# Another order of loads and of work for the first batch in a float32 kernel: relu(concat(x, mean, cond) @ W + b) + x on one core

## The chip, the core and the metric

The kernel runs on one core of a Trainium2 chip. The core has a matrix engine (TensorE, PE; its weight loads are PEld), a vector engine (VectorE, DVE), a scalar engine (ScalarE, ACT), GpSimd (POOL) and SyncE (SP), which here only issues transfers. Sixteen DMA engines move the data. The metric is the device time of one execution in microseconds, the median of several.

## The reference

Inputs: x (4, 1024, 512), cond_512 (4, 256), W (1536, 512), b (512), all float32. The two halves of the hidden vector are the same cond_512.

```
hidden = concatenate([cond, cond], axis=-1)                 # (4, 512)
x_mean = mean(x, axis=1, keepdims=True)                     # (4, 1, 512)
fused  = concatenate([x, x_mean * ones_L, hidden[:, None, :] * ones_L], axis=-1)
out    = x + relu(einsum('bld,do->blo', fused, W) + b)      # (4, 1024, 512)
```

The kernel takes W apart. W1 (rows 0 to 511) multiplies x. W2 (rows 512 to 1023) multiplies the mean over the 1024 positions, W3 (rows 1024 to 1535) the hidden vector: these two and b make one bias of 512 numbers for each batch, added inside the relu.

## The kernel before, in words

**Groups and tiles.** The 4 batches of 1024 positions are 8 groups g of 512 positions (LAST is 7). A group has 4 pieces k (128 of the 512 inputs), except group 0, which has 8 of half length: `pieces` is that list. It has 4 output tiles t of 128 outputs by 512 positions, and the last group has 8 half tiles (`tiles`, n counts them). Group g's output tile t is accumulated in bank t of `ps_y`, so there are four banks and each must be emptied before the next group's tile t begins.

**Precision.** x and W1 are each split into a high part and a rest (xh, xl, w1h, w1l), and a tile is three products for each k: w1h·xh, w1h·xl, w1l·xh (`product`, 12 matmuls of 512 columns a tile). Of W1, ACT makes the high part (L229) and POOL the rest (L201).

**A piece of x** goes: DVE turns it (32x32 transposes, `turn_x`, L300) into one of two banks of `ps_xt`; ACT rounds it to xh and sums it along the positions (`x_high`, L236, the sum is the mean's); DVE makes xl (`x_low`, L306), which frees the bank. xh and xl have four slots (SLOTS), so x may be turned three groups ahead.

**A bias** for batch b: DVE multiplies W2 with the sums (`mean_terms`, L329 to L334, the tile w2x), PE adds over the partitions (`mean_bias`, L425), and DVE adds the constant part and turns it (`sum_bias`, L346 and L349). The constant part (`ps_const`, L457, `const_row`, L372) needs W3, whose halves POOL adds (L215), cond spread on POOL (L212), and b. Both sums of a batch's two groups are needed, so the bias of batch b can be made only once its second group (2b + 1) is turned.

**A finished tile** goes: ACT adds the bias and takes the relu into `relu_t` (a ring of 8, L256), DVE turns it back (`turn_back`, L317), POOL adds it to x in place (L207; DVE in the last group, L342), SP stores a group of x (L187). Since bias 0 is late, the four tiles of group 0 are copied from `ps_y` to `relu_t` first (`save`, L242) and their relu is done there later.

**Order.** Each engine works through a list that is written out in the code. PE: group 0 with all w1h products first and the 16 w1l products last; tile 0 of group 1; then `ps_const` and the mean of batch 0; then tiles 1 to 3 of group 1; then group after group, tile t of group g behind the relu of tile t of group g - 1. The mean of batch b (b above 0) stands behind tile 2 of group 2b. DVE: groups 0 and 1, `mean_terms(0)`, one piece of group 2, bias 0, the rest of group 2, group 3, `mean_terms(1)`, and then the tiles, in which the pieces three groups ahead are interleaved. SP's loads go x0 (half), W1, x0 (half), x1, cond, W2, W3, b, x2, and x3 to x7 each behind the landing of an earlier group; ACT and POOL load the rest of W1. POOL's residual of tile n (`added`) frees a slot of `back` for `turn_back(n + 4)`.

**WARM** (L403): 14 matmuls on zeros run from the start, to 7.3 us.

## Time and profile before

| | |
|---|---|
| median of 3 runs | 114.72 us (114.51 to 115.58) |
| the profiled execution's own time | 114.67 us |
| its span | 112.9 us |
| PE busy | 99.7 us, 88% of the span |
| DVE / ACT / POOL busy | 82.9 / 48.2 / 46.0 us |
| all DMA | 20.08 MB, mean 178 GB/s |

The span is what the profile sees; 1.8 us of the execution lie outside it. Matmuls overlap, so that what one costs is the step from its start to the next one's start, 0.23 us for 512 columns and 0.12 us for 256, and not its own length. In a timeline, "idle before" is the engine's wait and the name behind the arrow what ended it.

### The profile page before, as it was taken

The page shows a single profiled execution, that of the slowest core. Times are in us where ns is not written, and L with a number is a line of the kernel's source. Part 1 is how long each engine was busy: PE and PEld are TensorE (multiplying, and loading weights), DVE is VectorE, ACT ScalarE, POOL GpSimd, SP SyncE. Part 2 cuts the span into 40 slices and gives each one's busy share as a digit, 9 for nine tenths or more (in the row PEclk, how much of TensorE's full clock was granted, in tenths as well). Part 3 has the DMA queues.
Part 4 walks back from the last instruction along what each step waited for, and adds up shares of the span by engine and source line. Part 5 has one row for each costly group of instructions (what it writes and reads, how often), then busy time and mean ns, then how long its engine had stood idle before and what let it go on. Part 6 is the DMA issues. An engine that isn't in the chain of part 4 may idle for free.

```text
span 112.9 us, 1832 instructions
## 1 busy us (share of the span) xinstructions
PE 99.7 (88%) x526; PEld 79.9 (71%) x526; DVE 82.9 (73%) x148; ACT 48.2 (43%) x118; POOL 46.0 (41%) x43
## 2 busy tenths in 40 slices
PE   5959999841999899999999999999999999999900
PEld 2319998521788588677888886888888868999900
DVE  1027849890278899999999992899999976797530
ACT  4148415910029985028738400595654006433310
POOL 5348400008000000099985620446666089980000
PEclk9999999998599999999999999999999999999995
DMA  2999999999999999994869539100391670687966
GB/s 82 259 239 231 218 203 237 339 261 219 221 219 218 223 219 222 219 217 84 198 178 226 144 76 253 43 0 0 76 252 43 160 211 6 136 234 179 255 142 171
DMA packets 36023, 20.08 MB, mean 178 GB/s; under 512 B 1968, under 2 KB 34864, under 8 KB 36016
## 3 DMA queue, kind: packets, MB, share of 16 engines
q1 hardware_dynamic: 34576, 18.69, 77.1%
q10 hardware_dynamic: 1248, 0.79, 2.6%
q0 software_dynamic: 192, 0.52, 1.8%
q8 instruction: 3, 0.05, 0.2%
q14 instruction: 4, 0.03, 0.1%
HBM read 11.60 MB, written 8.39 MB: 177 GB/s over the span
## 4 chain that ended last, share of the span: by engine, by line
PE 60%; SPq 17%; DMA 8%; ACT 5%; DVE 3%; issue 3%; DVEq 0%
PE ps_y L406 60%; DMA xa<-in_x_dram 8%; SPq L162 8%; ACT relu_t L256 3%; SPq L141 3%; SPq L171 2%; ACT xh L236 2%; SPq L175 1%; DVE ps_xt L300 1%; PE ps_mean L425 1%; SPq L169 1%; SPq L146 1%; SPq L173 1%; DVE back L317 0%; DVE xa L342 0%
## 5 line engine op out<-in xcount | busy, mean ns | idle before, releaser
L406 PE MATMUL ps_y<-xh,w1h 128*128 128x256 f32 (+2 forms) x160 | 52.9, 355 | 2.5 <-ACT xh L236 1.4
L406 PE MATMUL ps_y<-xl,w1h 128*128 128x256 f32 (+2 forms) x160 | 51.8, 348 | 0.0
L207 POOL TENSOR_TENSOR xa<-xa,back 128x512 f32 x28 | 35.7, 1303 | 37.5 <-DVE back L317 37.5
L406 PE MATMUL ps_y<-xh,w1l 128*128 (+2 forms) x144 | 50.5, 368 | 0.0
L406 PEld LDWEIGHTS ps_y<-xh,w1h 128*128 128x128 f32 x160 | 28.8, 191 | 9.2 <-issue 2.4
L256 ACT ACTIVATE relu_t<-ps_y,bias 128x512 f32<-128x512 f32 (+1 forms) x32 | 20.0, 633 | 31.2 <-DVE bias L349 22.0
L300 DVE STREAM_TRANSPOSE ps_xt<-xa 128x512 f32<-128x512 f32 (+1 forms) x36 | 22.2, 640 | 12.9 <-DMA xa<-in_x_dram 12.6
L406 PEld LDWEIGHTS ps_y<-xl,w1h 128*128 128x128 f32 x160 | 28.8, 191 | 3.6
L406 PEld LDWEIGHTS ps_y<-xh,w1l 128*128 128x128 f32 x144 | 27.2, 190 | 4.5
L236 ACT ACTIVATE xh<-ps_xt 128x512 fp32r<-128x512 f32 (+1 forms) x36 | 19.7, 548 | 23.3 <-DVE ps_xt L300 23.2
L306 DVE TENSOR_TENSOR xl<-ps_xt,xh 128x512 fp32r<-128x512 f32 (+1 forms) x36 | 22.3, 618 | 4.4 <-ACT xh L236 4.4
L317 DVE STREAM_TRANSPOSE back<-relu_t 128x512 f32<-128x512 f32 (+1 forms) x36 | 22.1, 630 | 3.9 <-ACT relu_t L256 3.7
L334 DVE SCALAR_TENSOR_TENSOR w2x<-w,bsum,w2x 128x512 f32<-128x512 f32 x12 | 9.0, 752 | 0.4
L403 PE MATMUL ps_mean<-warm 128*128 128x512 bf16 x14 | 6.1, 629 | 1.2 <-DVE warm L361 1.2
L236 ACT ACTIVATION_READ_ACCUMULATOR xh<-ps_xt 128x1 f32 x36 | 7.1, 197 | 0.0
L201 POOL TENSOR_TENSOR w1l<-w,w1h 128x512 fp32r<-128x512 f32 x4 | 5.0, 1280 | 3.9 <-ACT w1h L229 3.9
L215 POOL TENSOR_TENSOR w3sum<-w 128x1024 f32<-128x1024 f32 x1 | 2.4, 2417 | 8.2 <-DMA w<-in_L_cond_W_dram 8.2
L342 DVE TENSOR_TENSOR xa<-xa,back 128x256 f32<-128x256 f32 x8 | 5.1, 632 | 0.3
L403 PEld LDWEIGHTS ps_mean<-warm 128*128 128x128 bf16 x14 | 1.9, 145 | 4.5 <-issue 3.3
L457 PE MATMUL ps_const<-w3sum,cond_t 128*32 128x128 f32 x16 | 1.1, 419 | 4.1 <-POOL w3sum L215 4.1
L229 ACT ACTIVATE w1h<-w 128x512 fp32r<-128x512 f32 x4 | 2.4, 623 | 3.5 <-DMA w<-in_L_cond_W_dram 3.5
L457 PEld LDWEIGHTS ps_const<-w3sum,cond_t 128*32 128x32 f32 x16 | 0.7, 159 | 4.5 <-issue 4.5
(21 smaller groups left out, 19.5 us busy)
## 6 DMA issues: line engine op xcount, KB each, us to landing
xa<-in_x_dram SPq DMA_DIRECT2D x28, 256.0 KB, 6.7
out_dram<-xa SPq DMA_DIRECT2D x28, 256.0 KB, 3.5
xa<-in_x_dram SPq DMA_DIRECT2D x8, 128.0 KB, 5.9
w<-in_L_cond_W_dram SPq DMA_DIRECT2D x4, 256.0 KB, 6.8
w<-in_L_cond_W_dram SPq DMA_DIRECT2D x2, 512.0 KB, 9.7
w<-in_L_cond_W_dram POOLq DMA_DIRECT2D x4, 128.0 KB, 4.6
out_dram<-xa SPq DMA_DIRECT2D x4, 128.0 KB, 2.8
out_dram<-xa ACTq DMA_DIRECT2D x4, 128.0 KB, 2.4
```

The source lines that it names most:

```text
L162: sp.dma_start(xa[Q * j:Q * j + Q, g], xv[g, j]).then_inc(x_landed[h], 16)
L201: nc.gpsimd.tensor_tensor(as_tiles(w1l[:, k]), by_tile(w1[:, k]), as_tiles(w1h[:, k]), ALU.subtract).then_inc(w1l_ready, 1)
L207: nc.gpsimd.tensor_tensor(rows, rows, back[:, t], ALU.add).then_inc(added, 1)
L236: nc.scalar.activation(xh[:, g % SLOTS, k, l:l + nl], ps_xt[:, n % XT_BANKS, 0:nl], ACT.Copy, accum_out=xsum[:, part, k:k + 1]).then_inc(x ...
L256: nc.scalar.activation(relu_t[:, slot, 0:nl], products, ACT.Relu, bias=bias[:, g // H, t, g // H:g // H + 1]).then_inc(relu_done, 1)
L300: nc.vector.transpose(ps_xt[:, n % XT_BANKS, 0:nl], xa[:, g, l // Q:(l + nl) // Q, Q * k:Q * k + Q]).then_inc(xt_ready, 1)
L306: nc.vector.tensor_tensor(xl[:, g % SLOTS, k, l:l + nl], ps_xt[:, n % XT_BANKS, 0:nl], xh[:, g % SLOTS, k, l:l + nl], ALU.subtract).then_i ...
L317: nc.vector.transpose(back[:, t, 0:nl // Q], relu_t[:, n % RELU_RING, 0:nl].rearrange("p (lb om) -> p lb om", om=Q)).then_inc(turned_back, 1)
L334: nc.vector.scalar_tensor_tensor(out=w2x[:], in0=w2[:, k], scalar=bsum[:, k:k + 1], in1=w2x[:], op0=ALU.mult, op1=ALU.add).then_inc(w2x_st ...
L342: nc.vector.tensor_tensor(rows, rows, back[:, t, 0:nl // Q], ALU.add).then_inc(last_added, 1)
L403: nc.tensor.matmul(ps_mean[:], warm[:, 0:P], warm[:], start=True, stop=True)
L406: return nc.tensor.matmul(ps_y[:, t, ls], lhs, rhs, start=start, stop=stop, skip_group_check=True)
```

## The change

Five things are changed together.

1. **Loads at the start.** x0 and W1 are issued by SP (partition quadrants 0 and 1, `LOW`) and ACT (quadrants 2 and 3, `HIGH`); POOL issues none. W1 comes in pieces k = 0, k = 1, and k = 2 and 3. SP then loads alone: cond, x1, x2, W2, W3, b, x3 to x7, with no wait for a landing between them.
2. **cond** is loaded as 4 DMAs of 4 rows of 256 bytes into a zeroed tile and turned by DVE, instead of one DMA of 8-byte runs and a copy on POOL.
3. **Group 0 on PE**: the w1l products are interleaved with the others, as 32 matmuls of 256 columns instead of 16 of 512, and the last piece is done tile by tile.
4. **All 8 tiles of batch 0** (groups 0 and 1) are saved to `relu_t` (`SAVED`), so group 2 waits for `y_saved` and not for a relu.
5. **Order.** DVE turns group 2 before `mean_terms(0)`. PE does `ps_const` and the mean of batch 0 after all of group 1, and the mean of batch 1 in the middle of tile 3 of group 2, where it waits for bias 0 and w2x. Later means stand where they stood.

```diff
         @block.sync
         def _(sp):
...
-            load_x0(sp, 0)
-            load_w1(sp, 1, range(0, 2), w1_landed)
-            load_x0(sp, 1)
-            load_x(1, 1)
-            sp.dma_start(cond_c[:], cv).then_inc(cond_landed, 16)
-            for j in ORDER:
-                sp.dma_start(w2[Q * j:Q * j + Q], wv[1, j]).then_inc(w2_landed, 16)
+            load_x0(sp, 0, LOW)
+            load_w1(sp, 0, 1, LOW)
+            load_w1(sp, 1, 2, LOW)
+            load_w1(sp, 2, NK, LOW)
+            load_x0(sp, 1, LOW)
+            sp.wait_ge(cond_zeroed, 1)
+            for j in range(NQ):
+                sp.dma_start(cond_c[Q * j:Q * j + B], cv[j].rearrange("b (m k) -> b m k", k=CK)).then_inc(cond_landed, 16)
+            load_x(sp, 1, ORDER)
+            load_x(sp, 2, ORDER)
+            load_w2(sp, ORDER)
             for r in range(2):
                 sp.dma_start(w3[:, r], w3v[r]).then_inc(w3_landed, 16)
...
+            for g in range(3, G):
+                load_x(sp, g, ORDER)
...
         @block.scalar
         def _(act):
-            load_w1(act, 0, range(0, 2), w1_landed)
+            load_x0(act, 0, HIGH)
             act.wait_ge(ones_set, 1)
             nc.scalar.activation(act_warm[:], ones[:, 0:1], ACT.Relu)
+            load_w1(act, 0, 1, HIGH)
+            load_w1(act, 1, 2, HIGH)
+            load_w1(act, 2, NK, HIGH)
+            load_x0(act, 1, HIGH)
...
             def relu(n):
                 g, l, nl, t = tiles[n]
                 products, slot = ps_y[:, t, l:l + nl], n % RELU_RING
-                if g == 0:
+                if n < SAVED:
                     act.wait_ge(y_saved, n + 1)
                     products = relu_t[:, slot]
...
+            save(0)
+            x_high(pieces_to(H) - 1)
+            for n in range(1, NK):
+                save(n)
+            n_x = pieces_to(H)
+            x_high(n_x)
+            x_high(n_x + 1)
+            save(NK)
...
         @block.vector
...
-            turn_and_split(0, pieces_to(H))
+            turn_and_split(0, pieces_to(1))
+            dve.wait_ge(cond_landed, 16 * NQ)
+            nc.vector.transpose(cond_t[:], cond_c[:].rearrange("p m k -> p k m")).then_inc(cond_spread, 1)
...
+            turn_x(pieces_to(H))
+            turn_and_split(pieces_to(H), pieces_to(H + 1))
             mean_terms(0)
...
         @block.tensor
...
             for t in range(NK):
                 pe.wait_ge(y_saved, t + 1)
                 tile(1, 1, t)
...
+            pe.wait_ge(cond_spread, 1)
+            pe.wait_ge(w3_added, 1)
...
+            mean_bias(0)
+
+            for t in range(NK):
+                pe.wait_ge(y_saved, NK + t + 1)
+                for k in range(NK):
...
+                    if t == NK - 1 and k == NK // 2:
+
+                        pe.wait_ge(bias_ready, 1)
+                        mean_bias(1)
+                    last = product(H % SLOTS, k, t)
```

**On DVE, behind group 1** (the first x_low pair below is the end of group 1). Before, the mean of batch 0 comes straight behind it and x2 is turned around bias 0:

```order
L306 TENSOR_TENSOR xl<-ps_xt,xh 128x512 [waits xh_ready] x2
L323 TENSOR_TENSOR xsum<-xsum 128x4
L329 TENSOR_TENSOR bsum<-xsum 128x4 [waits halves_summed,w2_landed]
L331 TENSOR_SCALAR w2x<-w,bsum 128x512 [waits bsum_ready]
L334 SCALAR_TENSOR_TENSOR w2x<-w,bsum,w2x 128x512 [waits w2x_step] x3
L300 STREAM_TRANSPOSE ps_xt<-xa 128x512 [waits xl_ready,x_landed0]
L306 TENSOR_TENSOR xl<-ps_xt,xh 128x512 [waits xh_ready]
L372 TENSOR_TENSOR const_row<-ps_const,b_row 128x128 [waits b_landed,const_summed]
L346 SCALAR_TENSOR_TENSOR bias_row<-ps_mean,const_row 128x128 [waits mean_done,const_ready]
L349 STREAM_TRANSPOSE bias<-bias_row 128x128 [waits bias_summed]
L300 STREAM_TRANSPOSE ps_xt<-xa 128x512 [waits xl_ready] x2
```

With the change, from the end of group 2 on (its first row is the last x_low pair of group 2; line numbers are the changed kernel's):

```order
L303 TENSOR_TENSOR xl<-ps_xt,xh 128x512 [waits xh_ready] x2
L320 TENSOR_TENSOR xsum<-xsum 128x4
L326 TENSOR_TENSOR bsum<-xsum 128x4 [waits halves_summed,w2_landed]
L328 TENSOR_SCALAR w2x<-w,bsum 128x512 [waits bsum_ready]
L331 SCALAR_TENSOR_TENSOR w2x<-w,bsum,w2x 128x512 [waits w2x_step] x3
L372 TENSOR_TENSOR const_row<-ps_const,b_row 128x128 [waits b_landed,const_summed]
L343 SCALAR_TENSOR_TENSOR bias_row<-ps_mean,const_row 128x128 [waits mean_done,const_ready]
L346 STREAM_TRANSPOSE bias<-bias_row 128x128 [waits bias_summed]
L297 STREAM_TRANSPOSE ps_xt<-xa 128x512 [waits xl_ready,x_landed3]
```

All four pieces of x2 have moved ahead of the mean, and what follows bias 0 is now group 3, behind its landing.

**On PE, where the constant part stands.** Before, behind the last product of tile 0 of group 1:

```order
L406 MATMUL ps_y<-xh,w1l 128x512
L457 MATMUL ps_const<-w3sum,cond_t 32x128 [waits w3_added,cond_spread]
L457 MATMUL ps_const<-w3sum,cond_t 32x128 x7
L425 MATMUL ps_mean<-w2x,ones 32x128 [waits w2x_step]
L425 MATMUL ps_mean<-w2x,ones 32x128 x3
L406 MATMUL ps_y<-xh,w1h 128x512 [waits y_saved]
```

With the change, behind the last product of tile 3 of group 1 and ahead of group 2:

```order
L406 MATMUL ps_y<-xh,w1l 128x512
L471 MATMUL ps_const<-w3sum,cond_t 32x128 [waits w3_added,cond_spread]
L471 MATMUL ps_const<-w3sum,cond_t 32x128 x7
L425 MATMUL ps_mean<-w2x,ones 32x128 [waits w2x_step]
L425 MATMUL ps_mean<-w2x,ones 32x128 x3
L406 MATMUL ps_y<-xh,w1h 128x512 [waits xl_ready,y_saved]
```

36 matmuls of 512 columns (tiles 1 to 3 of group 1) now stand ahead of the wait for W3.

**On PE, tile 3 of group 2**, which has a wait in its middle that it did not have:

```order
L406 MATMUL ps_y<-xh,w1l 128x512
L425 MATMUL ps_mean<-w2x,ones 32x128 [waits w2x_step,bias_ready]
L425 MATMUL ps_mean<-w2x,ones 32x128 x3
L406 MATMUL ps_y<-xh,w1h 128x512
L406 MATMUL ps_y<-xl,w1h 128x512
L406 MATMUL ps_y<-xh,w1l 128x512
```

Before, the same four mean matmuls of batch 1 stood ahead of tile 3.

## Rows read from the trace of the kernel before

**Rows 1.** The page's busy times and one group of it; PE's waits (total, times, longest).

```profile
PE 99.7 (88%) x526; PEld 79.9 (71%) x526; DVE 82.9 (73%) x148; ACT 48.2 (43%) x118; POOL 46.0 (41%) x43
...
L229 ACT ACTIVATE w1h<-w 128x512 fp32r<-128x512 f32 x4 | 2.4, 623 | 3.5 <-DMA w<-in_L_cond_W_dram 3.5
...
PE ps_const L457 <- POOL w3sum L215: 4.1, 1, 4.1
PE ps_y L406 <- ACT xh L236: 1.4, 1, 1.4
```

**Rows 2.** The chain that ended last: start us, us, what.

```profile
39.13 8.46 PE ps_y L406 x36
47.60 0.36 PE ps_mean L425 x8
...
50.97 19.34 PE ps_y L406 x84
...
107.51 0.48 ACT relu_t L256
```

**Rows 3.** Timeline of PE: start us, us, engine, line, tiles, count, idle before.

```profile
1.21 6.11 PE L403 MATMUL ps_mean<-warm 128*128 128x512 bf16 x14 [1.21 <-DVE warm L361]
...
8.74 0.74 PE L406 MATMUL ps_y<-xh,w1h 128*128 128x256 f32 x4 [1.42 <-ACT xh L236]
...
20.85 0.50 PE L406 MATMUL ps_y<-xh,w1h 128*128 128x512 f32 x1 [0.48 <-ACT relu_t L242]
...
27.93 1.11 PE L457 MATMUL ps_const<-w3sum,cond_t 128*32 128x128 f32 x16 [4.07 <-POOL w3sum L215]
...
29.39 0.80 PE L406 MATMUL ps_y<-xh,w1h 128*128 128x512 f32 x1
...
31.17 0.39 PE L406 MATMUL ps_y<-xl,w1h 128*128 128x512 f32 x1
```

**Rows 4.** Timeline of DVE, ACT and POOL: the first users of x1, W3 and x2.

```profile
16.65 1.32 DVE L300 STREAM_TRANSPOSE ps_xt<-xa 128x512 f32<-128x512 f32 x2 [1.37 <-DMA xa<-in_x_dram]
...
20.20 0.59 ACT L242 ACTIVATE relu_t<-ps_y 128x512 f32<-128x512 f32 x1
...
25.36 2.42 POOL L215 TENSOR_TENSOR w3sum<-w 128x1024 f32<-128x1024 f32 x1 [8.21 <-DMA w<-in_L_cond_W_dram]
...
30.29 0.73 DVE L300 STREAM_TRANSPOSE ps_xt<-xa 128x512 f32<-128x512 f32 x1 [4.70 <-DMA xa<-in_x_dram]
```

**Rows 5.** Windows: stretch, length, busy by engine, PE clock, DMA share, GB/s.

```profile
15.00:16.00 1.00, 1.00 (x11) 1.00 (x10) 0.28 (x1) 0.00 (x0) 0.00 (x0) 1.00 1.33 181
...
26.00:30.00 4.00, 2.07 (x26) 1.63 (x27) 0.00 (x0) 0.00 (x0) 1.78 (x1) 0.70 1.22 220
```

**Rows 6.** Timeline of DVE from bias 0 to bias 1, and ACT's relu behind it.

```profile
32.38 0.28 DVE L372 TENSOR_TENSOR const_row<-ps_const,b_row 128x128 f32<-128x128 f32 x1
...
33.25 1.27 DVE L300 STREAM_TRANSPOSE ps_xt<-xa 128x512 f32<-128x512 f32 x2
...
38.28 1.31 DVE L300 STREAM_TRANSPOSE ps_xt<-xa 128x512 f32<-128x512 f32 x2
...
43.91 0.15 DVE L329 TENSOR_TENSOR bsum<-xsum 128x4 f32<-128x4 f32 x1
...
46.86 2.48 DVE L317 STREAM_TRANSPOSE back<-relu_t 128x512 f32<-128x512 f32 x4
...
49.98 0.69 ACT L256 ACTIVATE relu_t<-ps_y,bias 128x512 f32<-128x512 f32 x1 [6.14 <-DVE bias L349]
```

**Rows 7.** Timeline: SP's queue, which issues transfers, and ACT's table load.

```profile
0.76 1.85 SPq L141 DMA_DIRECT2D xa<-in_x_dram  x4
...
1.68 1.28 ACT L224 ACT_TABLE_LOAD   x1 [1.68 <-PEq L498]
...
5.60 4.66 SPq L162 DMA_DIRECT2D xa<-in_x_dram  x4
10.30 1.02 SPq L169 DMA_DIRECT2D cond_c<-in_cond_dram  x1
```

More of the change, by code:

```diff
@@ L62, in build @@
     tiles += [(LAST, l, HL, t) for l in (0, HL) for t in range(NK)]
+    SAVED = H * NK
     def steps_of_x(n, ahead):
-        return 1 if SLOTS <= tiles[n][0] + ahead < G else 0
+        return 1 if SLOTS <= n // NK + ahead < G else 0
     xv = x.rearrange("b (h lb lm) (j e) -> (b h) j lm lb e", h=H, lm=Q, j=NQ)
@@ L136, in build, with load_x0, load_x, load_w1 @@
         turned_back, added, last_added = sem("turned_back"), sem("added"), sem("last_added")
-        def load_x0(eng, half):
+        def load_x0(eng, half, quadrants):
             lbs = slice(half * LB // 2, (half + 1) * LB // 2)
-            for j in ORDER:
+            for j in quadrants:
                 eng.dma_start(xa[Q * j:Q * j + Q, 0, lbs], xv[0, j, :, lbs]).then_inc(x0_landed[half], 16)
-        def load_w1(eng, half, quadrants, landed):
-            ks = slice(half * NK // 2, (half + 1) * NK // 2)
+        def load_x(eng, g, quadrants):
             for j in quadrants:
-                eng.dma_start(w1[Q * j:Q * j + Q, ks], wv[0, j, :, ks]).then_inc(landed[half], 16)
+                eng.dma_start(xa[Q * j:Q * j + Q, g], xv[g, j]).then_inc(x_landed[g], 16)
+        def load_w1(eng, first, end, quadrants):
+            for j in quadrants:
+                eng.dma_start(w1[Q * j:Q * j + Q, first:end], wv[0, j, :, first:end]).then_inc(w1_landed[first], 16)
+        def load_w2(eng, quadrants):
+            for j in quadrants:
+                eng.dma_start(w2[Q * j:Q * j + Q], wv[1, j]).then_inc(w2_landed, 16)
         def store_last(eng, quadrants):
@@ L434, in _ @@
                         pe.wait_ge(w1h_ready, k + 1)
+                    if half == 1 and k == NK - 1:
+                        pe.wait_ge(xl_ready, NK * H)
+                        for t in range(NK):
+                            mm(t, ls, w1h[:, k, t], xh[:, 0, k, ls])
+                            mm(t, ls, w1h[:, k, t], xl[:, 0, k, ls])
+                            mm(t, ls, w1l[:, k, t], xh[:, 0, k, ls], stop=True).then_inc(y_ready, 1)
+                        break
                     for t in range(NK):
@@ L440, in _ @@
                         mm(t, ls, w1h[:, k, t], xl[:, 0, k, ls])
-            for t in range(NK):
-                for k in range(NK):
-                    if t == 0:
-                        pe.wait_ge(w1l_ready, k + 1)
-                    last = mm(t, slice(0, NL), w1l[:, k, t], xh[:, 0, k], stop=(k == NK - 1))
-                last.then_inc(y_ready, 1)
+                    if half == 0 and k > 0:
+                        group0_low(half, k - 1)
+                    elif half == 1:
+                        group0_low(half, k)
+                if half == 0:
+                    group0_low(half, NK - 1)
             for t in range(NK):
@@ L474, in _ @@
                     tile(H * b + 1, (H * b + 1) % SLOTS, t)
-            even_group(B - 1)
+                for t in range(NK):
+                    pe.wait_ge(relu_done, NK * (H * b + 1) + t + 1)
+                    tile(H * b + H, (H * b + H) % SLOTS, t)
+                    if t == 2:
+                        pe.wait_ge(bias_ready, b + 1)
+                        mean_bias(b + 1)
             for n, (g, l, nl, t) in enumerate(tiles):
```

133 lines of the change are left out of this document (52 added, 81 removed).

## The prediction

> **What bounds the kernel now.** I read the page first: PE is busy for 99.7 of 112.9 us and nothing else comes near [rows 1]. The chain that ended last says the same: from 50.97 us on it is PE without a gap down to 107.5, and then relu, turn and store of the last half tile [rows 2]. So behind 50.97 only PE's own work counts, and the change adds and removes none there. What can be won lies ahead of it, and the list of PE's waits shows where: 4.1 us for POOL's sum of W3, and 1.4 us at the start for the first xh [rows 1]. The timeline gives the gaps a place. PE starts real work at 8.74, though its zero matmuls end at 7.32 (1.21 + 6.11), waits 0.48 before 20.85, and waits 4.07 before 27.93 [rows 3]. After that long gap it is slow as well: the granted clock is 0.70 on the mean of 26 to 30 us [rows 5], 16 + 8 small matmuls take 1.46 us (27.93 to 29.39) and the next four big ones 1.78 us (29.39 to 31.17) [rows 3]. At full pace these are 24 x 0.045 = 1.08 us (eight take 0.36 [rows 2]) and 4 x 0.23 = 0.92 us. The clock's fall cost 1.24 us.
>
> Last, what do the waits hang on? DMA moves 220 GB/s at share 1.22 even while PE idles, in 26 to 30, so it isn't resting [rows 5], and the first users of x1 (16.65), W3 (25.36) and x2 (30.29) start as these land [rows 4]. The first 35 us are a race with one full stream.
>
> **The change part by part.** I walk PE through the changed order, with durations of this trace, up to the start of group 3, which in the old trace is at 50.97.
>
> Loads at the start. Group 0 can start when x0's first half and W1's k = 0 are there. Best case is 7.35, behind the zero matmuls. Worst case: ACT's ten issues, at the pitch of SP's (1.85 us for four), and the table load between them (1.3) [rows 7] hold ACT to 0.76 + 4.6 + 1.3 = 6.7, and two xh and one w1h, at most 0.62 each [rows 1], make it 8.6. Either way group 0 is 96 matmuls of 256 columns at 0.12 = 11.5 us, and ends at 18.9 to 20.1; the 16 more weight loads hide in that pitch. But PE doesn't go on then: tile 0 of group 1 waits for the copy of tile 0, which ACT has behind three xh of group 1, and that copy starts at 20.20 because x1 lands at 16.65 [rows 4]. The three MB up to x1 are the same as before. I move x1's landing by 0 to 0.3 us and take 0.1. The start's gain ends there: group 1 starts at 20.75 instead of 20.85.
>
> The Trainium skill, "DMA: Bandwidth & Descriptors", section "Issuing engines are not separate DMA queues", says that DMAs of several engines share the same 16 DMA engines and that several issuers save only issue time. By that rule x1 gains nothing from the second queue, as in my sum; a gain of the start that is kept is a rival below.
>
> cond. Its 512 runs of 8 bytes show as the dip at 15 to 16 us: 181 GB/s at share 1.33 [rows 5]. 41 GB/s missing over 1 us, and a smaller dip behind it, are 0.25 us of the stream. Sixteen runs of 256 bytes cost next to nothing: W2, W3 and x3 land 0.25 us sooner, bounds 0 and 0.5. The new wait for cond on DVE stands ahead of x1's first piece; it is issued in front of x1 and so comes ahead of it. The turn of 64 columns costs at most the 0.3 of bias' turn and hides in DVE's idle 1.37 us before 16.65 [rows 4]. If cond came late, DVE would hold x1 and all behind it.
>
> Group 1. 48 matmuls at 0.23 = 11.05 us: 20.75 to 31.8. Its four tiles are saved by ACT, which has only x2's four pieces beside them in that time; group 2's tiles find their banks free.
>
> W3 now stands behind x2. A group of x is 1.05 MB, at 220 GB/s 4.77 us [rows 5]. So W3 is there at 25.36 + 4.77 - 0.25 = 29.9, its sum is done 2.42 later at 32.3 [rows 4], and the constant part starts at 32.45 (0.15 behind it as now). PE waits 0.65 instead of 4.07, too short for the clock to fall, going by the gap of 1.42 that did no such thing [rows 3]. Then 24 small matmuls at full pace: 33.55. w2x of batch 0 is ready: x2 lands near 16.6 + 4.77 = 21.3, and with 5.63 for a group and 2.95 for the mean (below) DVE has x1 split at 22.2, x2 at 27.8 and w2x at 30.9.
>
> Group 2 up to the middle of tile 3: 42 matmuls, 9.7 us, 33.6 to 43.3. There PE waits for bias 0 (below: 34.5, no wait) and for w2x of batch 1.
>
> The DVE chain now decides. const_row to the next turn is 0.87 us (32.38 to 33.25) [rows 6], so bias 0 is there at 34.5. x3 closes the same amount of data as before: 30.27 + 4.77 = 35.0, less 0.25 and a little: L = 34.7. From the first turn of a group to the next bsum DVE took 5.63 us (38.28 to 43.91) with ACT mostly free. With relus between, three pieces took 5.03 (33.25 to 38.28), or 6.7 for four [rows 6]. Now a relu stands between any two xh; it is nearer the first, since only one stands there and not two, and I take 6.0. bsum at 40.7. From there the old trace needs 2.95 to the first turn_back (46.86) and, over four turn_backs and bias 1, 6.76 until the relu that frees bank 0 is done (49.98 + 0.69 = 50.67) [rows 6]. The changed order on this stretch is the same. So w2x is ready at 43.65 (PE waits 0.35 for it), PE does the mean (0.36) and six matmuls (1.4) and ends group 2 at 45.4; the relu is done at 40.7 + 6.76 = 47.5, and PE starts group 3 at 47.5 after 2.1 us idle.
>
> Behind that the order on all engines is as before, and DVE, which leads this restart, keeps its place ahead of PE. The stores begin sooner, behind the same loads.
>
> **The sum.** 50.97 - 47.5 = 3.5 us less. Cross-check: groups 1 and 2 are 96 matmuls of 0.23 and 24 + 8 small ones, 23.5 us of work. The old stretch 20.85 to 50.97 is 30.1, so 6.6 of it is waiting: 4.07, the clock's 1.24, and shorter ones. The new one is 23.5 + 0.65 + 0.35 + 2.1 = 26.6, from 20.75 to 47.4. Against the profiled run's 114.67 that is 111.2; its time is within 0.05 of the median.
>
> Bounds of the unknown: L 34.2 to 35.3; the pass 5.63 to 6.7. Group 3 starts at 46.6 to 48.8, the time is 110.3 to 112.5.
>
> **The rivals.**
> - *The clock falls in group 2's wait* (2.1 us). 4.07 idle did it, 1.42 did not [rows 3]; this one is between. Price 1.24 as above: 112.4. Chance 0.12.
> - *The data come sooner.* If the second queue brought x0, W1 and x1 forward as much as PE's gap of 1.42 [rows 1], all landings move by that and the chain with them: 111.2 - 1.4 = 109.8. For it: four transfers are issued at once at the start, two by each engine. Against: SP's first issue is at 0.76 in both, and four are out by 2.6 in the old trace already [rows 7]. Chance 0.15.
> - *W3 decides, not x3.* If W3 or its sum is late by 1 us more than I have it, bias 0 holds DVE instead of x3: 34.5 + 1 + 6.0 + 6.76 = 48.3, 112.0, inside the range. Chance 0.13.
> - *x3 is late, slower than before.* x3 to x7 are issued with no wait for a landing, so x4's traffic may run beside x3's. If x3 lands a whole load (4.77) later, group 3 starts at 52.2 and the time is 115.9. It decides from L = 39.3 on. For it: SP needed 4.66 us for four issues at 5.60 [rows 7], so the queue was full. Against: x1 and x2 landed in their turn although W2 and others stood behind them. Chance 0.04.
> - *Nothing is won*: DVE's chain is the limit in both kernels, and bsum would have to come at the old 43.91 [rows 6], 3.2 later than in my sum, say by a landing of x3 at 37.9; 114.4. Chance 0.04.
>
> **How the numbers follow.** The forecast has 0.52. Range: 109.6 (data sooner) to 112.8 (clock falls, and a little late). A measurement of this kernel can tell 1% from no change. Under 113.6 are all but the last two, and some part of these: faster 0.91, same 0.05, slower 0.04.
>
> **What the changed profile would show.** PE: group 1 at 20.4 to 20.9, with idle time before it for ACT's copy; ps_const at 32 to 33 after under 1.5 us of waiting; a short wait in tile 3 of group 2; a wait near 2 us for the relu before group 3 at 46.6 to 48.8, in a chain that runs through DVE and x3's landing; no window at clock 0.5. From there 56.5 us of gapless PE. Wrong would be: group 1 before 20 (data sooner), PE gapless up to group 3, or a DVE that waits for cond.

## The result, and the profile after

The changed kernel takes 111.15 us (median of 4, 109.17 to 112.69), against 114.62 us (114.12 to 115.58, 4) for the kernel before on the same chip. The ratio is 0.955, with a 95% interval of 0.943 to 0.967, so faster; it rests on the changed kernel's two executions with a mean granted clock of 0.989 and 0.996 (109.17 and 109.98; the other two, at 0.976, took 112.31 and 112.69, see a2), and puts the time at 0.955 x 114.62 = 109.5 us. The direction was forecast, and the mechanism except for the loads at the start; by this ratio the time lies 1.7 us below the 111.2 and just below the range's low end of 109.6.

The profiled execution took 109.98 us with a span of 108.2, which is 4.7 less than before. First the page of the changed kernel, with its busy times (share of the span) and instruction counts:

```profile
PE 97.4 (90%) x542; PEld 79.7 (74%) x542; DVE 85.4 (79%) x149; ACT 50.4 (47%) x122; POOL 43.5 (40%) x38
```

PE is busier by share, and 2.3 us less in all, because no stretch ran at half clock (which the prediction prices at 1.24 us) and the zero matmuls took 4.99 us for 6.11 [rows 3]. The chain of work that ended last, of the changed kernel (start us, us, what):

```profile
33.59 0.72 ACT relu_t L252
...
39.88 0.76 DVE w2x L331
...
42.21 2.40 DVE back L314 x4
45.25 0.70 ACT relu_t L252
46.25 19.33 PE ps_y L406 x84
...
102.78 0.48 ACT relu_t L252
```

As before, the end is one gapless PE [rows 2]. It begins at 46.25 instead of 50.97, 4.72 sooner, and that is the whole gain: 50.97 to 107.51 were 56.5 us, 46.25 to 102.78 are 56.5 too. Ahead of it the chain runs through DVE and ACT, not through PE. PE's timeline of the changed kernel (idle time before a row, and what ended it, in brackets) has the places that the prediction names:

```profile
7.07 0.71 PE L406 MATMUL ps_y<-xh,w1h 128*128 128x256 f32 x4 [0.89 <-ACT w1h L227]
...
18.76 0.28 PE L406 MATMUL ps_y<-xh,w1l 128*128 128x256 f32 x1
19.59 0.50 PE L406 MATMUL ps_y<-xh,w1h 128*128 128x512 f32 x1 [0.55 <-ACT relu_t L239]
...
31.04 0.67 PE L471 MATMUL ps_const<-w3sum,cond_t 128*32 128x128 f32 x16 [0.28 <-POOL w3sum L210]
32.29 0.43 PE L425 MATMUL ps_mean<-w2x,ones 128*32 128x128 f32 x8 [0.58 <-DVE w2x L331]
```

The wait of 4.07 for POOL's sum [rows 3] has shrunk to 0.28. The wait of 0.58 for w2x was not in my sum. DVE's timeline of the changed kernel, from x1 to bias 1, with the relu of ACT that frees bank 0:

```profile
15.40 1.32 DVE L297 STREAM_TRANSPOSE ps_xt<-xa 128x512 f32<-128x512 f32 x2 [0.64 <-DMA xa<-in_x_dram]
...
27.67 4.56 DVE L331 SCALAR_TENSOR_TENSOR w2x<-w,bsum,w2x 128x512 f32<-128x512 f32 x3
32.15 0.28 DVE L372 TENSOR_TENSOR const_row<-ps_const,b_row 128x128 f32<-128x128 f32 x1
32.86 0.29 DVE L343 SCALAR_TENSOR_TENSOR bias_row<-ps_mean,const_row 128x128 f32<-128x128 f32 x1 [0.43 <-PE ps_mean L425]
...
33.52 1.32 DVE L297 STREAM_TRANSPOSE ps_xt<-xa 128x512 f32<-128x512 f32 x2
...
39.17 0.15 DVE L326 TENSOR_TENSOR bsum<-xsum 128x4 f32<-128x4 f32 x1
...
42.12 2.48 DVE L314 STREAM_TRANSPOSE back<-relu_t 128x512 f32<-128x512 f32 x4
44.53 0.25 DVE L343 SCALAR_TENSOR_TENSOR bias_row<-ps_mean,const_row 128x128 f32<-128x128 f32 x1
44.82 0.31 DVE L346 STREAM_TRANSPOSE bias<-bias_row 128x128 f32<-128x128 f32 x1
```

```profile
45.25 0.69 ACT L252 ACTIVATE relu_t<-ps_y,bias 128x512 f32<-128x512 f32 x1 [4.27 <-DVE bias L346]
```

x1 is turned at 15.40, where it was 16.65 [rows 4]: 1.25 us sooner, against the 0.1 that I had taken. x3 is turned at 33.52 without a wait, right behind bias 0. And three instructions that took 0.75 each before take 4.56 together: the second of them takes 2.99, beside POOL's sum of the halves of W3.

```profile
28.45 2.99 DVE L331 SCALAR_TENSOR_TENSOR w2x<-w,bsum,w2x 128x512 f32<-128x512 f32 x1
```

```profile
28.50 2.40 POOL L210 TENSOR_TENSOR w3sum<-w 128x1024 f32<-128x1024 f32 x1 [16.26 <-DMA w<-in_L_cond_W_dram]
```

The windows of the changed kernel (stretch, length, busy by engine, PE clock, DMA share, GB/s) show where the data gained:

```profile
5.00:10.00 5.00, 4.10 (x28) 3.11 (x27) 2.65 (x8) 3.43 (x12) 2.86 (x3) 1.00 1.06 298
15.00:16.00 1.00, 1.00 (x10) 1.00 (x9) 0.60 (x1) 0.00 (x0) 0.00 (x0) 1.00 1.23 227
```

and the same of the kernel before, of the first stretch:

```profile
5.00:10.00 5.00, 3.58 (x16) 1.87 (x15) 2.00 (x6) 2.64 (x8) 2.50 (x2) 1.00 1.11 239
```

In 5 to 10 us DMA moved 298 GB/s instead of 239. That is 0.30 MB more, and at the 225 GB/s of the stretch behind it 1.3 us of the stream.

### The profile page after: what moved, and what is told of

Same layout as the page of the kernel before. It is cut to its first block, busy times and chain, and to the rows that moved or that the text cites. A ratio compares the mean times of both kernels' runs of the same rounds, so it can differ in the third digit from the quotient of the medians.

```text
span 108.2 us, 1750 instructions
## 1 busy us (share of the span) xinstructions
PE 97.4 (90%) x542; PEld 79.7 (74%) x542; DVE 85.4 (79%) x149; ACT 50.4 (47%) x122; POOL 43.5 (40%) x38
## 4 chain that ended last, share of the span: by engine, by line
PE 53%; DVE 18%; ACT 10%; DMA 7%; SPq 6%; issue 2%; ACTq 0%; DVEq 0%
PE ps_y L406 52%; DMA xa<-in_x_dram 7%; DVE w2x L331 6%; ACT xh L234 5%; ACT relu_t L252 3%; DVE ps_xt L297 3%; DVE xl L303 3%; DVE back L314 3%; SPq L152 2%; SPq L144 2%; ACT relu_t L239 1%; SPq L148 1%; SPq L177 1%; PE ps_mean L425 1%; DVE w2x L328 1%
## 5 line engine op out<-in xcount | busy, mean ns | idle before, releaser
L406 PE MATMUL ps_y<-xh,w1l 128*128 128x256 f32 (+2 forms) x160 | 51.9, 347 | 0.0
L406 PEld LDWEIGHTS ps_y<-xh,w1l 128*128 128x128 f32 x160 | 28.7, 189 | 3.9
L252 ACT ACTIVATE relu_t<-ps_y,bias 128x512 f32<-128x512 f32 (+1 forms) x28 | 17.3, 626 | 29.4 <-DVE bias L346 20.1
L331 DVE SCALAR_TENSOR_TENSOR w2x<-w,bsum,w2x 128x512 f32<-128x512 f32 x12 | 11.3, 938 | 0.4
L252 ACT ACTIVATE relu_t<-relu_t,bias 128x512 f32<-128x512 f32 x8 | 5.4, 720 | 2.2 <-DVE bias L346 2.2
L239 ACT ACTIVATE relu_t<-ps_y 128x512 f32<-128x512 f32 x8 | 4.5, 596 | 3.7 <-PE ps_y L406 3.7
L403 PE MATMUL ps_mean<-warm 128*128 128x512 bf16 x14 | 5.0, 533 | 1.2 <-DVE warm L358 1.2
L343 DVE SCALAR_TENSOR_TENSOR bias_row<-ps_mean,const_row 128x128 f32<-128x128 f32 x4 | 1.1, 281 | 3.3 <-PE ps_mean L425 3.3
```

What stands on the lines that cost most here:

```text
L239: nc.scalar.activation(relu_t[:, n % RELU_RING], ps_y[:, n % Y_BANKS], ACT.Copy).then_inc(y_saved, 1)
L252: nc.scalar.activation(relu_t[:, slot, 0:nl], products, ACT.Relu, bias=bias[:, g // H, t, g // H:g // H + 1]).then_inc(relu_done, 1)
L331: nc.vector.scalar_tensor_tensor(out=w2x[:], in0=w2[:, k], scalar=bsum[:, k:k + 1], in1=w2x[:], op0=ALU.mult, op1=ALU.add).then_inc(w2x_st ...
L403: nc.tensor.matmul(ps_mean[:], warm[:, 0:P], warm[:], start=True, stop=True)
L406: return nc.tensor.matmul(ps_y[:, t, ls], lhs, rhs, start=start, stop=stop, skip_group_check=True)
```

## The experiments

The theories. **A, my walk**: PE's stretch ahead of group 3 is set by DVE's chain from the landing of the data, and only the size of one landing was off. **B, the data**: the new start brings x1 and all behind it sooner by 1 us or more. **C, two engines on one memory port**: DVE's long w2x instruction is long because POOL adds W3 at the same time. **D, the clock**: the wait before group 3 lets it fall in some executions. Each ratio below is to the kernel before on the same chip, with its 95% interval. Where not said otherwise, the edit is made to the changed kernel.

**a0_again, the changed kernel once more, on the chip of the next ones.**

> The changed kernel once more, on the chip of the three runs beside it. Its executions so far took 109.17 and 109.98 us at a mean granted clock of 0.989 and 0.996, and 112.31 and 112.69 us at 0.976. If the clock can fall in PE's 1.83 us wait before group 3, the times here split again into about 109.2 to 110 and 112.3 to 112.7. If the split was chance of that chip, they lie together within 0.5 us.

Measured: 110.42 us (109.12 to 111.11, 4), ratio 0.960 (0.952 to 0.967). x1 is turned at 14.90 and group 3 starts at 45.41. The gain repeats, and so does x1's early landing. The four times fit neither outcome: they spread over 2.0 us, but the two at the lower clock (0.969 and 0.977) took only 110.92 and 111.11.

**a5_old_start, the old loads of x0 and W1 and the old cond** (parts 1 and 2 undone, with ACT's old order of its first roundings, except that x1 to x7 stay in the new order):

```diff
-            load_x0(sp, 0, LOW)
-            load_w1(sp, 0, 1, LOW)
-            load_w1(sp, 1, 2, LOW)
-            load_w1(sp, 2, NK, LOW)
-            load_x0(sp, 1, LOW)
...
+            load_x0(sp, 0, ORDER)
+            load_w1(sp, 1, range(0, 2), w1_landed)
+            load_x0(sp, 1, ORDER)
             load_x(sp, 1, ORDER)
+            sp.dma_start(cond_c[:], cv).then_inc(cond_landed, 16)
...
+            load_w1(pool, 0, range(2, NQ), w1_q23_landed)
```

> The changed kernel with parts 1 and 2 undone at the start: x0, W1 and cond are loaded as before (cond behind x1, copied by POOL); the order x1, x2, W2, W3, b, x3, the saved tiles, group 0's matmuls and the places of the means are the changed kernel's. This is the kernel that my sum described, in which x1 lands when it did before: x1 at 16.3 to 16.7, the constant part at 32 to 33, group 3 near 47.5, 111.0 to 111.5 in the executions whose clock holds. If the start's parts are worth nothing, it is 109.2 to 110.0 like the changed kernel.

Measured: 112.72 us (111.49 to 115.67, 10), ratio 0.979 (0.974 to 0.984). Its timeline of PE and DVE:

```profile
32.58 0.67 PE L470 MATMUL ps_const<-w3sum,cond_t 128*32 128x128 f32 x16 [0.79 <-POOL w3sum L214]
...
47.60 0.49 PE L405 MATMUL ps_y<-xh,w1h 128*128 x1 [1.88 <-ACT relu_t L253]
```

```profile
16.40 1.32 DVE L298 STREAM_TRANSPOSE ps_xt<-xa 128x512 f32<-128x512 f32 x2 [1.01 <-DMA xa<-in_x_dram]
...
34.86 1.32 DVE L298 STREAM_TRANSPOSE ps_xt<-xa 128x512 f32<-128x512 f32 x2 [0.57 <-DMA xa<-in_x_dram]
```

With the old start, x1 lands within 0.15 of my 16.55, x3 at 34.86 where I had 34.7, the constant part starts at 32.58 where I had 32.45, and group 3 at 47.60 where I had 47.5. So the walk from x1 on was right (A), and what it lacked was the start (B). The time is less clean: of the ten executions one kept its clock (0.998), and it took 111.97 for the 111.0 to 111.5 expected; the traced one took 112.92, of which 1.6 are the clock's (see a2), so 111.3 without. As for size, the new start is worth 0.979 - 0.955 = 2.4% or some 2.7 us by the two ratios, whose intervals together span about 0.7 to 4.7 us, and 1.35 us by the two traces (47.60 against 46.25). The rest between these two would be the clock, whose mean is under 0.983 in nine of this kernel's ten executions, against four of eight of the changed kernel's. Why it falls more often here isn't shown.

**b1_start_loads, the kernel before with the new loads of x0 and W1 alone; b3_loads_cond, with the new cond too.**

```diff
-            load_x0(sp, 0)
-            load_w1(sp, 1, range(0, 2), w1_landed)
-            load_x0(sp, 1)
+            load_x0(sp, 0, LOW)
+            load_w1(sp, 0, 1, LOW)
+            load_w1(sp, 1, 2, LOW)
+            load_w1(sp, 2, NK, LOW)
+            load_x0(sp, 1, LOW)
...
-            load_w1(pool, 0, range(2, NQ), w1_q23_landed)
-            load_w1(pool, 1, range(2, NQ), w1_q23_landed)
```

> The kernel before with one part of the change: x0 and W1 issued by SP and ACT, W1 in three pieces, nothing issued by POOL; all else, the old order of loads too, as before. In the kernel before the first user of x1 starts at 16.65, in the changed one at 15.40. If the start of the loads did that, x1 is turned at 15.4 to 15.7 here, W3's sum starts near 24.2 instead of 25.36, and the time falls by about 1.2 us (113.4). If cond's 8-byte runs (issued behind x1) or another part did it, x1 is turned at 16.4 to 16.7 and the time falls by 0.3 or less.

> The kernel before with two parts of the change: the new loads of x0 and W1, and cond as four small DMAs in front of x1, turned by DVE; the old order of all else. With the start's loads alone x1 was turned at 16.31 us, though 3.36 MB had come by 15.0, more than the 3.15 MB up to x1. If the 512 runs of 8 bytes that stand behind x1 in the queue hold x1's last packets up, x1 is turned at 15.0 to 15.6 here as in the changed kernel (15.40), and W3's sum starts by 24.6. If cond's form costs only its 0.25 us of transfer, behind x1, x1 is turned at 16.2 to 16.4 again. The wait for W3 stays (4 to 5 us) in both, and the clock falls as before, so the time is 113 to 114.

Measured: b1 114.55 us (113.04 to 115.49, 4), ratio 0.985 (0.976 to 0.993). b3 112.31 us (112.09 to 113.91, 5), ratio 0.982 (0.973 to 0.991), less than the 113 to 114 expected. The first use of x1 in b1 and then in b3, in DVE's timeline:

```profile
16.31 1.32 DVE L301 STREAM_TRANSPOSE ps_xt<-xa 128x512 f32<-128x512 f32 x2 [1.08 <-DMA xa<-in_x_dram]
```

```profile
15.73 1.32 DVE L300 STREAM_TRANSPOSE ps_xt<-xa 128x512 f32<-128x512 f32 x2 [0.86 <-DMA xa<-in_x_dram]
```

**a3_pool_w1, W1's upper quadrants issued by POOL again instead of ACT**, the new cond kept:

```diff
+            load_w1(pool, 0, 1, HIGH)
+            load_w1(pool, 1, 2, HIGH)
+            load_w1(pool, 2, NK, HIGH)
...
-            load_w1(act, 0, 1, HIGH)
-            load_w1(act, 1, 2, HIGH)
-            load_w1(act, 2, NK, HIGH)
```

> The changed kernel with one thing undone: quadrants 2 and 3 of W1 are issued by POOL again, in the new pieces. If POOL's queue cost the 1.15 us by which x1 comes sooner in the changed kernel, x1 is turned at 16.2 or later and the time rises by about 1 us. If cond's form or place did it, x1 stays at 15.2 to 15.6, and the time within 0.4 us of the changed kernel.

Measured: 111.51 us (110.59 to 113.14, 4), ratio 0.973 (0.957 to 0.989), whose interval overlaps the changed kernel's. x1 is turned at 15.92, between the two outcomes, and DMA moved 269 GB/s in 5 to 10 us. Group 3 starts at 47.33, 1.1 later than in the changed kernel.

Nine traces have the new loads and the new cond (after, a0, a1, a2, a6, b3, and a7, c1, c2 below). They turn x1 at 14.90 to 15.73, with a middle of 15.34. The old start (before, a5, b4) turns it at 16.65, 16.40 and 16.63, so that the two groups don't meet: the new start as a whole brings x1 about 1.2 us sooner. How this divides is much less sure. a3, which issues from POOL, is at 15.92, outside the nine by 0.2 only; b1, which has the old cond, is at 16.31. Each is one execution, against a scatter of 0.8. The bytes say more of the issuer: by 15.0 us, 3.10 to 3.14 MB had been moved with the old start, 3.23 in a3, and 3.36 to 3.57 in all that have POOL issue nothing.

Of cond they say little. Against b3, b1's x1 is 0.6 later. But SP issues the old cond only at 9.39 in b1, and by 9.4 b1 had already moved 0.11 MB less than b3 (2.08 against 2.19), which is half a microsecond of the stream. b1 had moved 3.68 MB when x1 was turned, more than the changed kernel's 3.48; but b3, without the 8-byte runs, had moved 3.69. So these runs don't show that cond's old form costs more than the 0.25 that the prediction gave it, nor that it holds x1's last packets back.

The later landings scatter as well. POOL starts its sum of W3 at 25.36 in the kernel before and at 23.97 in b4, which has the same loads. In b1, where 24.2 was expected if the start decided, it is 26.14; in b3 it is 24.92.

**a6_old_group0, the old order of group 0's w1l products** (part 3 undone):

```diff
-                    if half == 0 and k > 0:
-                        group0_low(half, k - 1)
-                    elif half == 1:
-                        group0_low(half, k)
...
+            for t in range(NK):
+                for k in range(NK):
...
+                    last = mm(t, slice(0, NL), w1l[:, k, t], xh[:, 0, k], stop=(k == NK - 1))
```

> The changed kernel with group 0's matmuls in the old order (all w1h products first, then 16 w1l products of 512 columns). PE starts group 1 when ACT has copied tile 0, and ACT has three pieces of x1 ahead of that copy, so x1's landing decides and not PE's order: group 1 starts 4.2 us behind the first turn of x1 as in the changed kernel (19.59 for 15.40), and the time is 109.1 to 110.2 in the executions whose clock holds. If the interleaving matters, group 1 starts later against x1 by more than 0.3 us and the time rises by as much.

Measured: 110.06 us (109.43 to 110.61, 4), ratio 0.959 (0.952 to 0.967), the same as a0's 0.960 within the intervals. Group 1 starts at 19.54 there and at 19.59 in the changed kernel. Part 3 is worth nothing that these runs show, because group 1 waits for ACT's copy behind x1, and group 3 for DVE. Parts 1 and 2 on the old kernel (b3) have a ratio of 0.982, parts 3 to 5 on the old start (a5) 0.979, all five 0.955. What parts 4 and 5 are worth singly isn't tested.

**a7_w_first, W2, W3 and b loaded ahead of x2, as the kernel before had it**:

```diff
             load_x(sp, 1, ORDER)
-            load_x(sp, 2, ORDER)
             load_w2(sp, ORDER)
...
-            for g in range(3, G):
+            for g in range(2, G):
```

> The changed kernel with one thing undone: SP loads W2, W3 and b ahead of x2. DVE still turns x2 ahead of the mean. x2 then lands near 28.9, DVE has it split at 34.5 and w2x of batch 0 at 37.5, and PE, through with group 1 at 30.7, waits near 6 us for it, long enough for the clock to fall (0.50 in a window behind it). Group 2 starts near 37.9 and not 32.64, group 3 near 51, and the time is 114.5 to 116.5. If the order of the loads matters little since the queue is full anyway, it stays under 111.

Measured: 116.66 us (116.19 to 117.83, 4), ratio 1.018 (1.010 to 1.027), 1 to 3% slower than before and just above the range expected. A row of DVE's timeline and one of PE's:

```profile
29.09 1.32 DVE L296 STREAM_TRANSPOSE ps_xt<-xa 128x512 f32<-128x512 f32 x2 [8.26 <-DMA xa<-in_x_dram]
```

```profile
38.08 0.66 PE L424 MATMUL ps_mean<-w2x,ones 128*32 128x128 f32 x8 [7.01 <-DVE w2x L330]
```

and a window of it, with the clock in the third column from the end:

```profile
34.00:42.00 8.00, 3.92 (x16) 2.87 (x17) 6.69 (x14) 3.93 (x11) 0.00 (x0) 0.50 1.19 231
```

DVE's new order (x2 turned ahead of the mean) makes everything wait for x2, so the load order has to go with it. Behind the wait of 7.01 for w2x PE runs at half clock until past 42 us, and group 3 starts at 52.75, for the 51 expected. With DVE's order as it is, the place of x2 in the stream decides between a ratio of 0.955 and one of 1.018.

**a1_w3_on_pe, no sum on POOL: PE multiplies both halves of W3 instead**, with 32 small matmuls for 16:

```diff
-            nc.gpsimd.tensor_tensor(w3sum[:], w3[:, 0], w3[:, 1], ALU.add).then_inc(w3_added, 1)
...
-                for k in range(CK):
+                for r in range(2):
+                    for k in range(CK):
```

> The changed kernel without POOL's sum of the halves of W3: PE multiplies cond with both halves (32 small matmuls instead of 16). In the changed kernel one of the three multiply-adds of w2x takes 2.99 us instead of 0.75, from 28.45 on, and POOL's sum runs from 28.50 to 30.90. Port theory (DVE and POOL both read two SBUF tiles, and the one that comes second waits): all twelve multiply-adds take 0.75, w2x of batch 0 is ready at 29.2, the mean follows the constant part with no wait, bias 0 is ready near 32.6 and not 33.5, and the time falls by 0.3 to 0.9 us, less if x3 has not landed by then. DMA theory (the load of W3 and b slows DVE): one multiply-add still takes near 3 us and bias 0 comes at 33.5.

Measured: 110.24 us (110.06 to 112.00, 6), ratio 0.956 (0.950 to 0.961). From its timelines:

```profile
27.30 2.33 DVE L329 SCALAR_TENSOR_TENSOR w2x<-w,bsum,w2x 128x512 f32<-128x512 f32 x3
32.89 0.29 DVE L370 TENSOR_TENSOR const_row<-ps_const,b_row 128x128 f32<-128x128 f32 x1 [3.26 <-PE ps_const L470]
```

```profile
30.39 2.13 PE L470 MATMUL ps_const<-w,cond_t 128*32 128x128 f32 x29
```

The three DVE instructions are short again, which bears C out, but the 0.3 to 0.9 us expected don't show (a0 on the same chip has 110.42 and 0.960): PE now spends over 2 us on the constant part, DVE waits 3.26 for it, and bias 0 comes at 33.85 instead of 33.5.

**c1_bias_first, DVE makes bias 1 behind the first turn_back instead of behind the fourth.** In the changed kernel w2x of batch 1 is ready at 42.12 and PE's mean is done in 42.40 to 42.75, but DVE turns four tiles back (2.48 us) before it makes the bias that group 3 waits for.

```diff
+                if n == 1:
+                    sum_bias(1)
...
-                    if n // NK % H == H - 1 and n // NK // H + 1 < B - 1:
+                    if n // NK % H == H - 1 and 1 < n // NK // H + 1 < B - 1:
```

> The changed kernel with one move on DVE: bias 1 is made behind the first turn_back and not behind the fourth. PE waits 1.83 us for the relu of tile 0 of group 2, and that waits for bias 1. Three turn_backs are 1.8 us, so that bias 1 should be there 1.6 us sooner (it then waits for the mean's matmuls) and PE goes on nearly without a wait: 108.2 to 108.6 with an unbroken clock, and no slower executions, since the wait in which the clock fell is gone. Rival: DVE is the next limit; what PE gains it loses at the mean of batch 2, which DVE has ready only 1.8 us early now, and the time stays near 109.5.

Measured: 108.79 us (107.98 to 109.91, 4), ratio 0.948 (0.935 to 0.960). Its timeline of DVE, and of PE:

```profile
42.06 0.70 DVE L314 STREAM_TRANSPOSE back<-relu_t 128x512 f32<-128x512 f32 x1
42.89 0.29 DVE L343 SCALAR_TENSOR_TENSOR bias_row<-ps_mean,const_row 128x128 f32<-128x128 f32 x1
43.21 0.31 DVE L346 STREAM_TRANSPOSE bias<-bias_row 128x128 f32<-128x128 f32 x1
```

```profile
44.65 0.49 PE L408 MATMUL ps_y<-xh,w1h 128*128 x1 [0.24 <-issue]
...
47.86 0.50 PE L408 MATMUL ps_y<-xh,w1h 128*128 x1 [0.21 <-ACT relu_t L252]
```

The wait of 1.83 before group 3 is gone and PE starts it 1.6 us sooner. Of this 0.5 is lost again by the mean of batch 2, 0.2 of it in the wait at 47.86; the time is a little above the 108.2 to 108.6 expected. That the DVE chain decided group 3's start (A) is shown by this. It is the fastest of all kernels here, by its median and by its ratio, though the intervals of its ratio and the changed kernel's (0.943 to 0.967) overlap.

**c2_w3_behind, c1 with POOL's sum of W3 held until w2x of batch 0 is done.**

```diff
+            pool.wait_ge(w2x_step, NK)
             nc.gpsimd.tensor_tensor(w3sum[:], w3[:, 0], w3[:, 1], ALU.add).then_inc(w3_added, 1)
```

> The kernel with bias 1 behind the first turn_back, and POOL's sum of W3 held until DVE has w2x of batch 0. With no overlap all twelve multiply-adds should take 0.75 us (port theory); w2x is ready near 29.5, the sum runs 29.6 to 32.0, and the constant part and the mean follow each other at 32.1 to 33.0. That is 0.2 us later than the 32.76 at which the mean ends with the overlap, so the time should be within 0.4 us of the kernel with bias 1 moved (107.98 to 108.79). If a multiply-add still takes 2.7 to 3 us, POOL's sum isn't its cause.

Measured: 109.72 us (109.00 to 111.47, 4), ratio 0.952 (0.945 to 0.960). Its timelines:

```profile
27.78 2.33 DVE L332 SCALAR_TENSOR_TENSOR w2x<-w,bsum,w2x 128x512 f32<-128x512 f32 x3
```

```profile
30.19 2.35 POOL L211 TENSOR_TENSOR w3sum<-w 128x1024 f32<-128x1024 f32 x1 [18.07 <-DVE w2x L332]
```

```profile
32.69 0.67 PE L474 MATMUL ps_const<-w3sum,cond_t 128*32 128x128 f32 x16 [1.77 <-POOL w3sum L211]
```

The same POOL instruction, put behind instead of beside, and DVE's three take 2.33 instead of 4.56. With a1 this settles C. The time, expected within 0.4 us of c1's, is 0.9 above it: PE waits 1.77 for the sum that was held, the constant part starts at 32.69 and not at 32.1, and group 3 at 45.61 instead of c1's 44.65.

Other traces have the two side by side, and the order decides who is stretched. A multiply-add that runs when POOL starts keeps its 0.75 (a2, a3, a5, a6, b4, c1, and before, at 24.83). The next one, issued during POOL's sum, takes 2.75 to 2.83 (a0, a2, a5, a6, b4, c1). POOL's instruction in turn takes 2.61, 2.74 and 2.75 where a running multiply-add still had 0.36 or more to go (a6, a3, c1), and 2.34 to 2.43 in the others. Only in the changed kernel's trace does the long multiply-add begin first, by 0.05.

**a2_fill, 8 zero matmuls in PE's wait before group 3**, so that the wait is filled whatever its cause. Nothing reads their results.

```diff
+            for _n in range(8):
+                nc.tensor.matmul(ps_const[:], warm[:, 0:P], warm[:], start=True, stop=True)
```

> The changed kernel with 8 matmuls on zeros (512 columns bf16, into the bank of the constant part, read by nobody) in PE's wait before group 3, which is 1.83 us; at 0.22 us each they end 0.3 us before PE is released. If the slower executions (112.3 to 112.7) are those in which the clock falls in that wait, they vanish here: all executions at 109.2 to 110.2, mean granted clock at 0.985 or above in all. If they come from elsewhere they stay, at 0.976, and the median doesn't move.

Measured: 110.40 us (109.86 to 110.64, 4), ratio 0.957 (0.951 to 0.963). All four clocks are at 0.987 or above, as expected, but three of the times lie above the 110.2, and the median is a0's 110.42: the filling gains nothing here. Theory D is about single executions. Those of the changed kernel took 109.17 and 109.98 at a mean granted clock of 0.989 and 0.996, and 112.31 and 112.69 at 0.976; a1's took 110.1 to 110.4 four times at 0.991 to 0.998 and 111.89 and 112.00 at 0.977 and 0.979. The trace of a1 is one in which it fell behind the wait. Its timeline, with its windows (clock in the third column from the end):

```profile
46.53 0.50 PE L404 MATMUL ps_y<-xh,w1h 128*128 x1 [1.77 <-ACT relu_t L250]
...
47.61 0.63 PE L404 MATMUL ps_y<-xh,w1h 128*128 x1
48.03 0.63 PE L404 MATMUL ps_y<-xl,w1h 128*128 x1
```

```profile
48.00:50.00 2.00, 2.00 (x6) 1.58 (x5) 2.00 (x5) 1.75 (x6) 2.00 (x3) 0.50 1.14 214
```

Behind 1.77 us of idling the step from matmul to matmul is 0.43 (1.2 GHz) instead of 0.23 until 50.17. Twelve matmuls take 46.53 to 50.97, 4.44, which is 1.6 more than twelve at 0.23 and the 0.1 of a first one. a5's trace shows the same behind 1.88 us. The traces of the changed kernel, a0, a3 and a6 have waits of 1.77 to 1.87 at the same place and stay at 2.4 GHz, and so do b4 and c2 behind 1.84 and 1.77 us elsewhere. So such a wait lets the clock fall or not. Over all executions of kernels with the wait before group 3 (the changed kernel, a0, a1, a3, a5, a6), 17 of 32 have a mean clock of 0.982 or less. Of the twelve without it (a2, c1, c2) one has, at 0.980 and 111.47 us, in c2, which has its wait of 1.77 before the constant part. That fits D. But only a1's and a5's traces show where the clock fell; for the changed kernel's own four low executions it is inferred from their mean, and a0's are less cleanly split than a1's.

**b4_fill_before, the kernel before with 18 zero matmuls in its 4.07 us wait.** This asks what the clock's fall, which I had priced at 1.24 us, was worth.

```diff
+                    for _n in range(18):
+                        nc.tensor.matmul(ps_const[:], warm[:, 0:P], warm[:], start=True, stop=True)
```

> The kernel before with 18 matmuls on zeros (3.9 us at full clock, results read by nobody) in PE's wait of 4.07 us for W3's sum. The wait stays, the granted clock should not fall: no window at 0.5 between 27 and 33, and the time lower by the clock's price, which I put at 1.24 us: 113.2 to 113.6 for 114.6 to 115. If the slow matmuls behind the wait had another cause, the time stays or rises by the few tenths by which the zeros may run over.

Measured: 114.57 us (113.26 to 115.45, 10), ratio 0.995 (0.990 to 1.000). From PE's timeline and windows:

```profile
23.73 4.06 PE L453 MATMUL ps_const<-warm 128*128 128x512 bf16 x18
...
38.84 0.49 PE L406 MATMUL ps_y<-xh,w1h 128*128 x1 [1.84 <-ACT relu_t L256]
```

```profile
26.00:30.00 4.00, 4.00 (x39) 2.44 (x37) 1.63 (x3) 0.00 (x0) 0.32 (x1) 1.00 1.22 224
```

The clock stayed at 1.00 where it had been 0.70 [rows 5], PE was through group 1 sooner, and then it waited 1.84 for the relu before group 2, where the kernel before has 0.50. Group 2 starts at 38.84 instead of 39.13, and DVE turned x2 at 29.99 instead of 30.29, sooner by as much. DVE's chain from x2's landing decided that start all along, and the clock's fall was hidden behind it.

## Why the prediction was right and wrong

**What bounds the kernel.** Right. The gapless stretch behind group 3's start is 56.5 us in both, and the gain is the shift of its start.

**Loads at the start.** This is the step that failed, in the sentence "I move x1's landing by 0 to 0.3 us and take 0.1" and in the one behind it, "The start's gain ends there". It measured 1.25 us. The term was taken from "The three MB up to x1 are the same as before". The bytes are the same, the rate is not: 239 GB/s in 5 to 10 us of the kernel before, where the changed kernel moves 298. I read rates only at 15 and at 26 us and held the stream to be full. The window of 5 to 10 us would have warned me by its DMA share, 1.11 for 1.22 later, but not by its rate, which is above the later 222; that 298 could be moved there, only a run could show. Group 1 was to start when the copy of tile 0 let it, and it did so at 19.59 with 0.55 idle, instead of at 20.75, since the copy hangs on x1 as I had said. "Group 1 before 20 (data sooner)" was the prediction's own sign for this. Group 0 started at 7.07, ahead of my best case of 7.35, because the zero matmuls ended at 6.18 and not at 7.32; nothing came of that.

Beside this step stood a rule of the Trainium skill, "DMA: Bandwidth & Descriptors", section "Issuing engines are not separate DMA queues": several issuers save only issue time. The traces do not bear it out for this start as a whole: by 9.4 us it had moved 2.08 to 2.21 MB in ten traces (2.04 in a3, where POOL issues half of W1), against 1.85 to 1.88 with the old one. As the pieces and their order changed too, how much is the issuers' isn't separated.

**cond.** I took 0.25 (bounds 0 and 0.5) for all landings behind it, by the bandwidth that its dip takes. The runs don't measure it: b1's x1 is 0.6 behind b3's, but 0.5 of that lay there before the old cond was issued. The new wait of DVE for cond costs nothing: it turns cond at 14.52 in the changed kernel, and x1 only at 15.40.

**Group 1, W3 and the constant part.** Right in kind. W3 was used at 28.50 where I had 29.9, 1.4 sooner, and the wait was 0.28 for my 0.65. The clock held. But this landing scatters: the sum starts between 26.91 and 29.07 in five traces with these loads (after, a0, a2, a6, c1). Under the old start, a5 has 32.58 for my 32.45.

**w2x of batch 0.** I had it ready at 30.9 and PE without a wait. It was ready at 32.2, though DVE had turned x2 sooner than I thought, since the POOL sum of W3 now ran beside it. One SCALAR_TENSOR_TENSOR took 2.99 us instead of 0.75 while POOL's 2.40 ran, and PE waited 0.58. Before, the sum came at 25.36 [rows 4], when DVE's last multiply-add (24.83 to 25.58) was already running. I had moved both and not looked at whether they now meet. What it cost is an estimate: from the start of the constant part to bias_row it is 1.82 us here and 1.07 in c2, so it held bias 0 up by at most 0.75, and by less if x3 landed after 32.8.

The Trainium skill has this case: "SBUF — State Buffer", section "Who interferes with whom", says that a DVE instruction with two SBUF inputs contends with a GpSimd instruction that reads SBUF, and that the issue order decides who blocks. The traces agree: 2.99 beside the sum, 0.75 without (a1, c2), and in six more the one issued second is the one that is stretched (see c2).

**x3 and the pass.** I had DVE wait for x3 until 34.7. It didn't wait: bias 0 held it until 33.52. So in the rival's words W3's side decides and not x3, only sooner than in my numbers, because both had come sooner. The two are close: in a2 and a5 DVE waits 0.61 and 0.57 for x3. My low bound for group 3, 46.6, took x3 at 34.2 and forgot that my own bias 0 stood at 34.5; it should have been 46.9. The pass of group 3 took 5.65 (33.52 to 39.17), not 6.0: the relus between cost nothing.

**From bsum to group 3.** 6.76 was right: bsum at 39.17, relu done at 45.94, 6.77. Then PE starts 0.31 later, which I left out. The wait is 1.83 for my 2.1.

Together: 47.5 becomes 46.25 by -1.18 (bias 0 at 33.52 for x3 at 34.7), -0.35 (the pass), +0.01 and +0.31, but for 0.04 of rounding. The first term is the start's: with it undone, x3 is at 34.86.

**The rivals.** *The data come sooner* is what happened, with 1.25 for the 1.4 that I gave it, and 109.98 in the profiled execution for its 109.8. Its chance of 0.15 was too low, because my argument against it looked at when issues are out and not at what moves. It stood as the low end of the range, and the low end was this one case alone. *The clock falls in group 2's wait* also happened, as far as mean clocks tell, in about half of the changed kernel's executions. I had it as one outcome for the kernel; it is one for each execution. These two partly cancel in the plain median of 111.15, which lies at my 111.2 without bearing my sum out. *W3 decides* holds in the sense above. The other two did not occur.

**The clock's price.** I used 1.24 as a part of the gain in the cross-check ("6.6 of it is waiting: 4.07, the clock's 1.24, and shorter ones"). b4 shows that in the kernel before it was worth at most 1%, by its ratio about 0.5%, since DVE's chain covered it. The sum itself was right, as it went by the DVE chain.
